# A four-block model on one core: causal maxima split before a mask, reciprocals used two chunks later, and a scratch moved from PSUM to SBUF

## The reference, cut to what matters

```python
# block A: causal attention over 1024 tokens, 32 query/key heads of 4 channels
att = einsum('bhtd,bhsd->bhts', q * hd ** -0.5, k) / sqrt(hd)
att = softmax(where(causal, att, -inf))
att = att[:, :, 0] - lambda_full * att[:, :, 1]
out = einsum('bhts,bhsd->bhtd', att, v)          # then rms norm, w_proj, residual

# block B: for each token and each of 16 heads, causal attention of 64 queries over 64 keys
# where a query, a key and a value are single numbers (Q, K, V: 16 x 64 per token)
scores = einsum('bshq,bshk->bshqk', Q, K)
w = softmax(where(triu(ones((64, 64)), 1), -inf, scores))
attn = einsum('bshqk,bshk->bshq', w, V)          # then @ Wo + bo, residual
```

## Time and profile before

| | |
|---|---|
| median of three executions | 2318.2 us |
| profiled execution, its time | 2317.29 us |
| profiled execution, its span | 2315.6 us |
| busy in the span: TensorE, VectorE, ScalarE, GpSimd | 81%, 82%, 45%, 62% |
| block A (`phase_a2`) | about 105 to 700 us |
| block B (`phase_b`) | about 780 to 2255 us |
| one tile of block B (1102.55 to 1192.90 us): VectorE, TensorE, GpSimd busy | 86.95, 77.83, 78.24 us |
| VectorE idle until ScalarE's reciprocal (L982) | 54.4 us in 17 waits |
| TensorE idle until GpSimd's split (L460) | 25.2 us in 16 waits |

### The profile page before, as it was taken

One profiled execution on the slowest core, in us unless ns is written; L12 is line 12 of the kernel. 1 busy time (PEld: TensorE's weight loads), 2 busy tenths in 40 slices (PEclk: granted clock), 3 DMA queues, 4 the chain that ended last, 5 costly groups with the idle time before them and its releaser, 6 DMA issues. The chain is left out here.

```text
span 2315.6 us, 35954 instructions
## 1 busy us (share of the span) xinstructions
PE 1877.9 (81%) x14226; PEld 1394.4 (60%) x14226; DVE 1890.4 (82%) x1551; ACT 1045.0 (45%) x1408; POOL 1444.3 (62%) x673
## 2 busy tenths in 40 slices
PE   2291799999985678988888889889889888898886
PEld 1140344444434467777777777778777777777785
DVE  6370577777745499999999999999999999999984
ACT  1050466666671135444444444444444444535440
POOL 8120122222220188897987987988978979879871
PEclk9695899999996589999999999999999999999996
DMA  2011000000000000000000000000000000000000
GB/s 79 16 25 26 8 7 8 9 7 7 7 1 0 0 1 1 1 1 2 1 1 1 1 1 1 1 1 1 1 1 1 1 1 1 1 1 1 1 1 18
DMA packets 10618, 14.24 MB, mean 6 GB/s; under 512 B 4416, under 2 KB 7392, under 8 KB 10336
## 3 DMA queue, kind: packets, MB, share of 16 engines
q1 hardware_dynamic: 8928, 11.33, 1.8%
q10 hardware_dynamic: 1536, 0.61, 0.1%
HBM read 4.57 MB, written 1.05 MB: 2 GB/s over the span
## 5 line engine op out<-in xcount | busy, mean ns | idle before, releaser
L1042 POOL TENSOR_TENSOR b_p_ring<-b_p_ring,b_m 128x2048 f32<-128x2048 f32 (+7 forms) x384 | 1250.9, 3293 | 207.4 <-DVE b_p_ring L951 206.1
L1074 ACT ACTIVATE b_p_ring<-b_p_ring 128x2048 f32<-128x2048 f32 (+7 forms) x384 | 535.7, 1412 | 777.1 <-POOL b_p_ring L1042 775.5
L1134 PE MATMUL b_ps<-k_ident,b_ev_ring 128*128 128x128 f32 (+6 forms) x4608 | 596.3, 281 | 148.2 <-DVE b_ev_ring L1000 144.4
L1000 DVE TENSOR_TENSOR b_ev_ring<-b_p_ring,b_ps 128x2048 f32<-128x2048 f32 (+7 forms) x384 | 633.2, 1653 | 3.1 <-PE b_ps L1100 1.6
L1134 PEld LDWEIGHTS b_ps<-k_ident,b_ev_ring 128*128 128x128 f32 (+6 forms) x4608 | 503.8, 138 | 217.9 <-DVE b_ev_ring L1000 192.9
L951 DVE TENSOR_TENSOR b_p_ring<-b_ps,b_key 128x2048 f32<-128x2048 f32 (+7 forms) x384 | 633.4, 1657 | 0.0
L1134 PE MATMUL b_ps<-k_ident,b_p_ring 128*128 128x128 f32 (+6 forms) x4608 | 579.2, 277 | 15.6 <-ACT b_p_ring L1074 9.5
L1134 PEld LDWEIGHTS b_ps<-k_ident,b_p_ring 128*128 128x128 f32 (+6 forms) x4608 | 514.4, 137 | 24.4 <-ACT b_p_ring L1074 10.2
L562 DVE TENSOR_REDUCE a_negm<-a_ps 128x1 f32<-128x768 f32 (+7 forms) x384 | 350.4, 953 | 192.7 <-PE a_ps L451 188.5
L545 ACT ACTIVATE a_ex<-a_ps 128x512 f32<-128x512 f32 (+3 forms) x768 | 333.1, 498 | 300.0 <-PE a_ps L490 291.7
L361 POOL TENSOR_SCALAR_AFFINE_SELECT a_ex<-a_ex 128x512 f32<-128x512 f32 x128 | 81.3, 635 | 439.0 <-ACT a_ex L545 437.5
(11 more groups left out here) (157 smaller groups left out, 1037.1 us busy)
## 6 DMA issues: line engine op xcount, KB each, us to landing
rk<-rows_k SPq DMA_DIRECT2D x384, 8.0 KB
rq<-rows_q SPq DMA_DIRECT2D x192, 16.0 KB
k_wqkv<-in_wqkv SPq DMA_DIRECT2D x1, 2048.0 KB, 8.4
out<-x_all SPq DMA_DIRECT2D x4, 256.0 KB, 2.4
k_wo<-in_wo SPq DMA_DIRECT2D x1, 512.0 KB, 9.2
k_w_attn<-in_w_attn ACTq DMA_DIRECT2D x1, 192.0 KB, 2.5
k_reset_max<-in_reset_max ACTq DMA_DIRECT2D x1, 128.0 KB, 4.8
k_reset_min<-in_reset_min SPq DMA_DIRECT2D x1, 128.0 KB, 9.0
```

What stands on the lines that cost most here:

```text
L1000: nc.vector.tensor_tensor(chunk(ev_ring, c), chunk(p_ring, c), over_queries(values(c), c), ALU.mult).then_inc(ev_done.sem, 1)
L1042: nc.gpsimd.tensor_tensor(pc, pc, over_rows(m[:, half].rearrange("p i h -> p (i h)"), c), ALU.subtract).then_inc(shifted.sem, 1)
L1074: nc.scalar.activation(pc, pc, ACT.Exp).then_inc(exp_done.sem, 1)
L1134: last = nc.tensor.matmul(ps[0:width, bank, b // IB * P:(b // IB + 1) * P], rows[:, r, b:hi].rearrange("p i h -> p (i h)"), k["ident"][:], ...
```

## The change

Three edits. In block A seven `max` units are done early instead of five, five of them ahead of `rows` instead of three, and GpSimd's `split` moves from behind the mask of group 9 to ahead of it. In block B `finish`, `project`, `residual`, `keys`, `take_key`, `keys_by_head` and `scans` all move two chunks later. The result of L974 goes to a new SBUF tile `by_minimum` instead of `T_BANK`; so the last operation of `maxima` has two SBUF inputs instead of one in PSUM and one in SBUF, VectorE no longer waits for `key_taken` there, and TensorE's `keys_by_head` waits for `key_taken` instead of `m_step`.

```diff
-        EARLY, EARLY_ROWS, TURN_ITEM = 5, 3, 6
+        EARLY, EARLY_ROWS, TURN_ITEM = 7, 5, 6
@@ phase_a2, GpSimd
                 for at in DIAGONAL:
+                    if at == 9 and n + 1 < JOBS:
+                        split(n + 1)
                     mask(n, at)
                     if at == 2 and n >= 1:
                         combine(n - 1)
-                    if at == 9 and n + 1 < JOBS:
-                        split(n + 1)
@@ phase_b
-    FINISH0_AT, FINISH1_AT, PROJECT_AT, RESIDUAL_AT = 19, 3, 4, 6
-    XT_AT, KEY_AT, KEY_TAKEN_AT = 5, (7, 9), (10, 12)
-    HJ_AT, SCAN_AT = (13, 15), (14, 16)
+    FINISH0_AT, FINISH1_AT, PROJECT_AT, RESIDUAL_AT = 21, 5, 6, 8
+    XT_AT, KEY_AT, KEY_TAKEN_AT = 5, (9, 11), (12, 14)
+    HJ_AT, SCAN_AT = (15, 17), (16, 18)
@@ phase_b, tiles
+        by_minimum = sb("by_minimum", [P, FIRST, H])
@@ phase_b, VectorE, maxima
-                t = ps[:, T_BANK].rearrange("p (i h) -> p i h", h=H)
-                if half == 1 and not last:
-                    dve.wait_ge(key_taken.sem, key_taken.at(it + 1, 2))
                 nc.vector.tensor_tensor(m[:, half], q, at(kmax), ALU.mult).then_inc(m_step.sem, 1)
-                nc.vector.tensor_tensor(t, q, at(kmin), ALU.mult).then_inc(m_step.sem, 1)
+                nc.vector.tensor_tensor(by_minimum[:], q, at(kmin), ALU.mult).then_inc(m_step.sem, 1)
                 dve.wait_ge(m_step.sem, m_step.at(it, 3 * half + 2))
-                nc.vector.tensor_tensor(m[:, half], t, m[:, half], ALU.max).then_inc(m_step.sem, 1)
+                nc.vector.tensor_tensor(m[:, half], by_minimum[:], m[:, half], ALU.max).then_inc(m_step.sem, 1)
@@ phase_b, TensorE
-                            pe.wait_ge(m_step.sem, m_step.at(it, 6))
+                            pe.wait_ge(key_taken.sem, key_taken.at(it + 1, 2))
```

## The result

The changed kernel took 2331.29 us (median of five executions, 2328.05 to 2334.62), the kernel before beside it 2317.31 us: a ratio of 1.0063 (95% interval 1.0047 to 1.0079), 14 us slower. The profiled execution took 2334.62 us, with a span of 2332.9 us. In its rows the scan is on L959 and L961, `maxima` on L971, L972 and L974, the product on L952, `finish` on L980, the values on L998, `shift` on L1040, the sums on L1132 and the projections on L1097 and L1098.

What follows compares the result with a forecast made beforehand. VectorE was taken to bound block B, busy 86.95 of 90.35 us a tile. 2317.3 - 12 (block A) + 9 (block B) = 2314.3 us, median 0.9 above: 2315 us; own range 2303 to 2327, no-change band 2311.2 to 2325.2.

Steps and rivals of the forecast that it cites:

- rival 2: Block B: TensorE becomes the bound behind the blocked `maxima` operation, its clock falling in nearly every tile; 2331 us; 16%.
- The stall: Block B, ahead of `finish`: its 3.24 us in the tile shown go, and 0.08 us with them.
- The scratch: Block B, second half's last `maxima` operation: VectorE blocked until 0.56 us after GpSimd's chunk 15; next product 0.65 us later.
- Block A: The earlier split removes 0.77 + 18.9 us of TensorE's waits, new costs 1.7 + 5 + 1.1: -12 us (-17 to -5).
- (b): Block A, behind `rows`: VectorE needs 4.6 us for what TensorE issues in 4.2; 0.4 us a job, 13 jobs +5.
- (a): Block A: three scores and one `values` now stand behind TensorE's 66 us wait for job 3's keys: +1.7 us.
- (c): Block A, job 14: group 9's mask waits for the last unit and split; wait 3.8 us instead of 2.69: +1.1.
- block B: All of block B: +3 us for stall and scratch, 6 us for TensorE's clock; +9 (+2 to +18).
- I take 0.4 us a tile, 6 us, since some of the loss may fall into the idle time itself: Block B, TensorE's lower clock after about 5 us idle: chosen between bounds of 0 and 15 us.
- The first tile: Block B: no stall there; VectorE waits 2.25 us for chunk 14's end, 2.12 more than now, less 0.61: +1.5 us.
- The middle and last tiles: Block B without the clock: +0.04 us a tile, +0.6 for tiles 1 to 14, and +0.65 for the last.
- Rival 1: Block B: VectorE's last `maxima` operation isn't blocked, or hardly, by GpSimd: -50 us, time 2256 us; 12%.

Runs made afterwards that it cites:

- e7: The changed kernel with 24 useless transposes of the unit matrix on TensorE between the sums of chunks 12 and 13 in block B: 2318.16 us, ratio 1.0004.
- e5: The kernel before with only GpSimd's split moved ahead of the last mask in block A, early units unchanged: 2300.79 us, ratio 0.9935.
- e1: The changed kernel with the scratch of `maxima` back in PSUM, all else as changed: 2258.05 us, ratio 0.974.
- e2: The kernel before with the scratch of `maxima` in SBUF and nothing else changed: 2340.39 us, ratio 1.0096.
- e9: The changed kernel, scratch in SBUF, with GpSimd's chunk 15 made to wait for `maxima` of the second half: 2270.95 us, ratio 0.9808.

## Why the prediction was wrong

The forecast was 2315 us, within 0.3%; it came to 2331.3 us, slower, with the mechanism and the time of rival 2.

Right, with sizes. *The stall* ahead of `finish` is gone. *The scratch*: the operation takes 4.16 us in the tile shown, where 4.0 were counted (1134.75 to 1138.80). The row for its end behind GpSimd, 0.56 us from L131, held at 0.54 and 0.55 us. Where the clock behind the block stayed at 1.00 (e7) a tile takes 90.5 us, and the prediction's terms without the clock make 90.4. *Block A* gained 9.05 us where -12 stood with bounds of -17 and -5. Its job was to take 30.8 us and took 30.82, partly by luck: by e5 the split alone gains 1.73 us a job (31.96 less 30.23) instead of 1.57, and the early units cost 0.59 instead of the 0.4 of (b). Short were (a), 2.35 instead of 1.7 us (252.71 less 251.13, plus the 0.77 gained), and (c): from the `rows` ahead of the last job to the last it was 33.4 us (668.06 - 251.13 - 12 x 31.96) and is 36.0 (658.55 - 252.71 - 12 x 30.82), 2.6 us more instead of 1.5 (the 1.1 of (c) and the 0.4 of (b)).

Wrong was the size of block B, +9 instead of +26.3 us. Of these 17.3 us 10.0 are the clock and 7.3 the tiles without it; block A adds 3 to the miss. Times from the last operation of the first half's `maxima` to the next tile's, in us; the last tile up to its `residual`:

| | first tile | 14 middle tiles | last tile | sum |
|---|---|---|---|---|
| before | 84.20 | 1263.79 | 97.95 | 1445.94 |
| changed | 91.93 | 1280.91 | 99.37 | 1472.21 |
| changed, TensorE filled (e7) | 90.21 | 1266.82 | 99.23 | 1456.26 |
| changed, scratch in PSUM (e1) | 84.75 | 1217.86 | 94.62 | 1397.23 |

- The step that failed is "I take 0.4 us a tile, 6 us, since some of the loss may fall into the idle time itself". Between the second and third row lie 16.0 us, 1.0 us a tile. The pieces of that step were right or near: five us idle (4.2), a clock between its two levels, 1.7 us of work lost, and an order that just fits at full clock. One was miscounted without harm: from 1143.3 on TensorE has seven long sums and one short, not six and two; with three projections these make the 16.7 us it says. Only the last factor was read from no row, and rows 8 spoke against it: there the low clock came in the windows behind the idle one, as it does now (0.69 and 0.88 behind 1138 to 1142, whose own clock was 1.00). A granted 0.69 and 0.88 is (0.31 + 0.12) x 4 = 1.7 us of work, and 1.7 us is what the sums took longer: nothing of the loss fell into the idle time.
- The first tile: 6.0 us (e7) instead of 1.5. "VectorE waits 2.25 us for the end of chunk 14" was to be followed by `maxima`, but GpSimd went straight on to chunk 15 and VectorE waited for that too. The rest is 1.06 us of waiting for the second half's queries, which the prediction overlooked.
- The middle and last tiles, without the clock: 3.0 and 1.3 us instead of 0.6 and 0.65. Most of the difference is the `finish` that left the rest of the tile: from the second half's `maxima` to the next first half's VectorE takes 30.41 us, end to end, in e7 where it took 30.87, 0.46 less and not 0.61. Why isn't shown.

The Trainium skill, "SBUF — State Buffer", section "SBUF: two separate sides", has whichever of the two starts first hold the shared pair for its whole instruction, and the other fully blocked. That agrees with all 15 later tiles: L974 ends 0.55 us behind GpSimd's chunk 15, 2.2 to 4.2 us after it was ready, where sharing would have cost it at most its own 0.69 us again. In the first tile the blocked operation lost twice, which the rule as it stands doesn't tell.

Rival 2 was given 16% and its price for the scan was the right one, 1.0 us (0.95 us in the tile shown, 0.86 to 1.50 elsewhere). That its 2331 us is what was measured is partly luck: it had +3 for the rest of block B, which was 10.3, and perhaps 0.3 us a tile for the queries, for which VectorE waits in no later tile. The prediction itself had its condition, "as soon as the clock falls", and a row for the fall; the condition should have had most of the chance. It came true in eleven of the 14 middle tiles. Rival 1, an operation that isn't blocked, has the time that the scratch in PSUM gives: e1 measured 2258 us where it said 2256.

## What to carry to other kernels

A stall that disappears from the list of waits can come back as busy time: compare the mean duration of each group before and after, not only the waits. If a VectorE operation has two SBUF inputs and stands beside a busy GpSimd, moving one input to PSUM can save it most of a GpSimd instruction, here 73 us in all for 16 operations. Where no bank is free, let GpSimd wait a moment for the short operation rather than VectorE for the long one (60 us here). And a wait of TensorE, even where it is not the bound, has a second price, the clock behind it: charge the whole loss to the work that follows, and look whether another engine has slack for it. In e7 the slack ahead of L974 took up 1.8 us; ahead of the scans there was none.

## What the runs showed of the hardware

- A VectorE instruction with two SBUF inputs that waits for GpSimd isn't let in between two of GpSimd's instructions that follow each other without a gap: it was ready at 858.30 us, 1.04 us ahead of the end of chunk 14 (863.88 less 4.54), and ran only behind chunk 15. In e2 it took 7.27 us at the same place. Where GpSimd waited for a semaphore between the two (e9), it took 1.65 us. In the trace before, 0.06 us between two of GpSimd's casts was enough: L131 with two SBUF inputs began at 43.62 us, after the first cast had started (43.36), and ended at 44.60, 0.55 us behind that cast's end, while the second cast ran until 45.07.
- Useless work sped the kernel up: 2.6 us of useless transposes a tile kept TensorE's clock at 1.00 ahead of the scans and gained 13 us.
- The length of one wait alone doesn't tell whether TensorE's clock falls. At the place behind the block, in the changed kernel, it fell with all twelve waits of more than 4 us and with one of the four of 2.28 to 2.41 us; in e7 it did not with those of 1.54 to 1.61 us, nor with one of 3.46 us in the first tile (869.8), but did with one of 2.86 us in the last (2226.9). In e9 it fell with the 2.27 us ahead of 1416.92.
